# Perceiver stack of four layers: x of the cross attentions turned by VectorE's blocks and through DRAM instead of by TensorE

## The chip, the cores and the metric

One core of a Trainium2 chip runs the whole program. TensorE multiplies matrices (and can turn a 128x128 tile by multiplying it with the identity), VectorE, ScalarE and GpSimd work elementwise, and SyncE (SP) issues the DMAs. The engines each run their own stream of instructions in order and wait for each other by semaphores. The metric is the device time of one execution in microseconds; the smaller the better.

## The reference

The input x is 64 sequences of 64 tokens with 128 features; a context of 64 x 128 x 96 and a mask come with it. Four layers follow one another, each with a cross attention to the context, a self attention and a feed forward part (in layers 0, 2 and 3 one that routes tokens to experts). Every part starts with a layer norm of x and adds its result to x. What the change touches is the start of three cross attentions:

```python
# layer 0 (x is the visual side, ctx the text side); the result has 128 columns, one for a context row
xn = layernorm(x)                                        # each token over its 128 features
v = einsum('bsd,hd->bsh', xn, Wv) + bv                   # 64 features
t = einsum('bsd,hd->bsh', ctx, Wt) + bt
x = x + einsum('bih,bjh->bij', v, t) / maximum(norm(v)[:, :, None] * norm(t)[:, None, :], 1e-8)
# layers 2 and 3: attention with 16 heads of 8 features
q = layernorm(x) @ Wq + bq ;  k = ctx @ Wk + bk ;  val = ctx @ Wv + bv
x = x + project(softmax(q k^T / sqrt(8)) val)            # layer 2 also clips the scores; layer 3 projects by a small MLP
```

TensorE contracts over partitions. x lies in SBUF with tokens on partitions, so for q the normed x has to be turned, so that its features lie on partitions (for the first product of layer 0 as well).

## The kernel before, in words

x stays in SBUF from first to last, 32 tiles of 128 tokens. Each of the 12 parts ("blocks", L0x, L0a, L0f, L1x, ... L3f; x is a cross attention, a a self attention, f a feed forward) is cut into jobs, mostly of 4 tiles (512 tokens), so 8 jobs for each of L0x, L2x and L3x, 24 in all. Two contexts, each with its own rooms in SBUF and four of the eight PSUM banks, take one job after another by PLAN. Their jobs run interleaved on the same engines, so that the one fills the other's waits.

A job is a set of programs, one for an engine, cut into steps by `yield`. The order in which all steps of both contexts are issued is a string written out in the code, ORDER, of 8,321 characters: a letter is the next step of one program (small letters context 0, capitals context 1), a digit ahead of a letter of TensorE's is a number of filler matmuls, identity times a constant, that the step issues where it has `pe_warm` (L467), and a plus loads the weights of a later block. Since each engine works in order, a wait in one step holds back all that the string puts behind it on that engine, the other context's steps too.

Each job has main programs (PROGRAMS: p for TensorE, a for ScalarE, g for GpSimd, v for VectorE) and early ones (EARLY_PROGRAMS), which may run while the job before in that context is still at work: d, VectorE's sums of the norm (L501); l, GpSimd's power of -1/2 (L489); k, ScalarE's normed x, written to xn (L509); and q, the DMA of the context, ctxT (L530). Each context has two early rooms, used in turn.

The main part of L2x and L3x starts with `pe_context` (L1875). TensorE makes the keys (L1882) and the values (L1887) from ctxT, then turns the four tiles of xn with four transposes into one PSUM bank (`pe_turn`, L463). ScalarE copies the bank to SBUF as xT (`act_turned`, L479), in act_context (L1900). TensorE then multiplies xT with wq (L1897), ScalarE adds the bias. Meanwhile VectorE spreads the keys over four lanes into kx (L1768) and adds the bias to the values, va (L1931, L2062). In L3x it makes qx from q as well. In L0x it is the same with other names: pe_L0x (L542) multiplies ctxT (L552), turns xn, and multiplies xT with wv (L564). Both routines also use `pe_turn` and a bank elsewhere; only the turn of xn is touched.

The expert blocks use SP for another thing: the routing weights are written to DRAM (`sp_keep`, L847) and read back spread over the partitions (L865, L879, L882). These are the s steps.

Of the kernel before, what the change touches and what calls it, by code (L numbers as in the profile page):

```python
# [12 lines left out]
P = 128  # L13
S = 64
D = 128
CX = 96
SC = 128
# [223 lines left out]
class Context:  # L241
# [4 lines left out]
    def __init__(self, nc, number, psum):  # L246
        self.nc, self.number, self.psum = nc, number, psum
        self.named, self.tally = {}, {}
# [21 lines left out]
class Job:  # L270
# [3 lines left out]
    def __init__(self, core, k, name, group, context, turn, first):  # L274
        self.core, self.k, self.name, self.group, self.context, self.turn, self.first = core, k, name, group, context, turn, first
        self.tiles = TILES.get(name, 4)
        self.seqs, self.tok, self.ctok = 2 * self.tiles, self.tiles * P, 2 * self.tiles * SC
        self.psum, self.c, self.half = context.psum, core.c, core.half
        self.m = {**core.rooms[name][context.number], **core.early_rooms[name][context.number][turn % 2]}
        self.x = core.x[:, group * self.tiles:(group + 1) * self.tiles, :]  # L280
        self.warm = 0
        self.base = {n: count for n, count in context.tally.items() if n[:-1] in EARLY}
# [41 lines left out]
    def free_early(self, engine, source=False):  # L324
# [5 lines left out]
        for number, count in done.items():  # L330
            if count > 0:
                engine.wait_ge(self.core.contexts[number].sem("done"), count)

# [187 lines left out]

def early_room(r):
# [19 lines left out]
def pe_L0x(nc, j):  # L542
# [45 lines left out]
def act_L0x(nc, j):  # L588
# [6 lines left out]
    yield  # L595
    s.wait_ge(*j.at("turned", 1))
    act_turned(nc, j, m["xT"][:], 0).then_inc(*j.up("features"))
# [1277 lines left out]
def pe_context(nc, j):  # L1875
# [15 lines left out]
    t.wait_ge(*j.at("normed", 1))  # L1891
    t.wait_ge(*j.at("k_ready", 1))
    pe_turn(nc, j, 0, m["xn"])
    yield
    pe_warm(nc, j, 1)
    t.wait_ge(*j.at("features", 1))
    t.matmul(psum[:, 1, :], j.weight("wq"), m["xT"][:], start=True, stop=True).then_inc(*j.up("queries"))  # L1897


def act_context(nc, j):  # L1900
# [6 lines left out]
    yield  # L1907
    s.wait_ge(*j.at("turned", 1))
    act_turned(nc, j, m["xT"][:], 0).then_inc(*j.up("features"))
# [34 lines left out]
def pe_L2x(nc, j):  # L1944
# [8 lines left out]
    t.wait_ge(*j.at("features", 2))  # L1953
# [51 lines left out]
def act_L2x(nc, j):  # L2005
    yield from act_context(nc, j)
    yield
    nc.scalar.wait_ge(*j.at("turned", 2))
# [113 lines left out]
def act_L3x(nc, j):  # L2122
    s, m = nc.scalar, j.m
    yield from act_context(nc, j)
    yield from act_waves(nc, j, SC, 1)
# [677 lines left out]
def sp_L3f(nc, j):  # L2803
# [18 lines left out]
EARLY_PROGRAMS.update({name: {"q": sp_early_context, "d": dve_early, "l": pool_early, "k": act_early} for name in ("L0x", "L2x", "L3x")})  # L2822
# [11 lines left out]
EARLY_BYTES = 6528  # L2834

# [5 lines left out]
    "vqQDDddDVdldkdddp8paglPLaDKQqDpDDLPaApgApGp7PvvdDavAkGKvvpPPP1paVVa3pgdAdaVpgdVlVPp1pA2PGvQvA4PDadvAkPGPlPvdvkV1pVa3pDDA"  # L2841
    "dLdvvDavvadavlVKpVvVPPAApGQPvvvA1PlvGvPvvdPDgkdVv9pVgAaVVVPpApGpapaDpaDLapDKQppvvpPaApDvavvaPavDkdpddDLA1PvlGpPvDvKvPvVV"
    "vAvvVgldVvVP5PAG1pAQDPapDAGPPaPpVDVLpgAVaaVDVPppakppKDpDDdvLvp1PaApDAGvva4PavavApkGPvPdpdPvvvVdvlVvAKVvvVgVLv+P1pVgAPaVD"
    "AVVApAVpdKDPpVpaaDPkpVVDaVLpapDVKVpVvVvGpLVa4pdPDpbArdrpKrdrlrPrrrGPrrrPrrArPArAPrArrPrrPaPVdvVPcApbPsaDVsVApAVsADpVDsvp"
    "LPsavgpVpgaPvgcVVgVpVcaVkcVpVGcVpvPaDpgApKvLPgaPGPPAAPAPAPPVDVPpApPaVVAcAAcpKDVVvDgPvgcVcPv1pVVVaVpVpbVpVdGpaDrLrVpavPGr"
    "pArrrLPrdrrPDrArrPKrrDdrlPrrAPrrrAvPAPPacVbVPpAspKDvPsaVsDVADpdsLAVpAVspvDgPagpVgpaKvgPcVgkVVpVcaVpVcVGcVcvGPvpAgPagPPAL"
    "APAPAPPPVVPpAcvPgVDAVVcAAVcKvpPqdDapVpbrPrrrarpVrVrprrdrvpardVplrvpaVprvprVarpvparVrprdVrGrvpaVcpbDvsPaDpdLApvsGDdPsdPAl"
    "PsAdPAsKPgPkPgAcgPacgkVcVgc+DPgpAcvgDcgPPBRRcdRRDRAcLRRPvRPqRRdpVPaRARpRpRRaRPdRdRRRpDvvCVpBASaaPgaSPvgVPSAlvPVSPAvgPSVP"
    "APVGvPAvPGdPpGpapaCaVGACkGpCGvCVGvdaCGCKvCddvlCVPpAaPvDpdBRPaRkRDpRRRDRvpapRpRadqRRdpRaRRRgpdRRRARRadvPaCVgPBvSPlAvPdvkV"
    "gSdPAPVSPALSvPvpdSpVapaPdaGApVGCvGCvaPGPlvvPGDApaPdvAkVpGPapAvppadqdapddvlpadVgpaGvPaCVKgdCGvCvdCgCCvvV1PAppapaakpPvPdvl"  # L2850
    "aPPvv1pBRRadvdpRRRARRAPVakRpVvpPaqdRpRAdDpaRdpRalRvgRRpaRDddRPDRaRdRdCVgPvBSlPvAvPgVSPAPVSPAvSvppdapSaPaGk1pGCvPGvaCGCvv"
    "GCVApaLCvVGpPGakpvpPAdqdavpDdpVadlpaGdpaKdgdvCaCgCvvVPAgDPdDPBDRPRRLvARvplpaRpRaPdRaRVkpRRRARPvPRRvRaPDRVRPRRvRvCdApBaPS"
    "vkpSapSvppaVApqdaddlpaSdgVpavGSvPGaPAgPvCAvdkgPdKVCdVPPlAvvpGpdapaPaGpAGCvGCvVaCGCvvCpaPvkpa1pvppadqdapvddVpaGpagvCaVPgA"
    "1PQlvvPgBRDPRRdPdAkdAv3pvpRaVpaPRaRRRpDRDLPvPvRaRVRDPdlvv1pdRAaPvkVpRdRPDaDpRDLDvppaapRARRvKpdapdaVgARvCaPBgPVSPAvKPvVSg"
    "DPdSSlv9pvSpapaPaGA1pAGCvGCvaGPCGvdvGpaCvkpa1pvvpdCaVpdGVpvGCvCvCvgV+VPgpQADdaPvPvDPpDvAVpAAGPvgAlvpGLVpaVdDpVGaapVp1PvP"
    "ADpkVDvAvPvvA2PvpVpaKpaappvVDvALvv6pVVDvpPaKpVpAvpvPvAvgPdgpddvV4PPAaDPQvDPvVADpAAPvGADvpLGDpaDgpVDaDVLaVpGpv3plvVvv5PvA"
    "vpVpPaDdPApAa1PapVpVAvkvvVv7pDVvpPaKpVKpvAvPvAvPgV1PpQDAgpPvPavDPvVApAAPvDvpLgDpaADGpGVadapVdpVGv3pDvvDvLV3PvPAvpdVplaPA"
    "pAa1PapVpVAvDdvkvv6pDVVvpPaApVpvPvAKvPpKvgVPQvgAPDPDDvaLPpDvdApAAPvGKvpdpVaDAdpDlVaGapVVdpGv3pvvVDvL3PvgPDvpVpaPApAAa1Pa"
    "pVpVAvvkvVv9pVPvADpVavdKpvvvPaavvAvvPvvvvdvvvdvVPPAAPlvQDPvAvvDvDpvLAPaGDvdpAvKVpGVVpVaDGkvDpapVVPPDvApgPvpLaAgApPvagpVp"
    "VvApDgpVVpvvvpPaApKVvvvPDaavvA1PvvvvvdvvvVPPAAPvQvPvAvvvGDpPDavAvDdLvVVpADvvpGVpVaGpapVvpVgPvPAPADpgaDADdlpadPkvgpVpVLvA"  # L2860
    "pgpKVDVpDvvvpPaKpVAvvvPdaavvAvdPvvvvvvvvdVPPAAPlvQvvPvAvvVGvDpAPavVDpAvDpGLVpDVvaGDpapVdDVPpAvPDgvPApALakgPpVapVvApDgpKV"
    "VDPvAgpVKPpAPVPAvvvpPPAaPADqGPADVdpVADddvGvvalVavvVvGvvvvvvvvvvvvvLVp1PvaVDvpvAvPPdApAPapVvVpApvaVgVKppkvgPaApVaPvgpApvP"
    "gpV+DPpVADp2PvvPVvVqpVVGPapPVGvVApVDvLagPv1pVaVPg3PdnAPzmAzzPwy6nwwAdPyVny2nVxVPdzlzV2mVG1nxVmzxmwzw3mzPyw7PwwAnxP3mynxy"
    "mnx2mAzznwDAPzKPw6mzVVVVwPzwVPAyPwPdVxnVPyVmVGnxDVGymDVx2mAnPww1mDzLzV4nGwPwwzx7mzzVy5nxVPDymnxmynwPwzzApPakpAvpAqddPaPp"
# [12 lines left out]
    "PrrvrrrrarrdVPrprAvPrkVGkPpAcpa1PabVspAvvsNpZspaMZZpQavYWggcvgWcgcWGcXcNvDpdYMdNXYMaNX1MZZNWWDMZ1pZZaWpYWWpavXNvpdvlY3Mv"
    "lgvNXgaMY1NXMWZW2MDZvNgWpLWWppZXp2MZdZYpvXNvMYvX3MaNWWvMYpWNaZWZ2NWaXZpZZMvYppv1NvXvvvpYMvDvNvXMYKNW1pWZZPvA2PgvVPvDgvPA"
# [213 lines left out]
```

## Time and profile before

| | us |
|---|---|
| three runs, median | 2554.51 |
| lowest and highest run | 2552.6, 2557.82 |
| profiled execution, span from the first to the last instruction | 2557.4 |
| TensorE busy | 2254.9 (88%) |
| VectorE busy | 1746.6 (68%) |
| ScalarE busy | 1368.6 (54%) |
| GpSimd busy | 774.0 (30%) |

The profiled execution has no other time on its page than its span; it lies inside the spread of the runs. A busy share is that of the whole span, over blocks with different limits. TensorE's contains the fillers (L471, 588 of them). L0x runs from about 20 to 130 us, L2x from 787 to 1433, L3x from 1632 to 2298; other blocks run beside them. The mean granted clock of TensorE is 0.971 of full speed.

### The profile page before, as it was taken

To read this page: it belongs to the slowest core of one execution; us is meant where nothing else is said; L and a number is where in the kernel's file an instruction comes from. 1 tells how busy PE (TensorE), PEld (TensorE's weight loads), DVE (VectorE), ACT (ScalarE), POOL (GpSimd) and SP (SyncE) were. 2 spreads that over 40 slices of the span, in tenths; PEclk is the share of its full clock that TensorE was granted. 3 is DMA by queue.
4 is the path that set the end of the run, shared out by engine and by line. 5 is a ranking of instruction groups with operands and counts; after the bars stand their busy time and mean duration, and the time that the engine had idled before them with its cause. 6 is when DMAs were issued, how large, how long until landed. Compare 5 with 4: busy or idle time off the path is not lost.

```text
span 2557.4 us, 62072 instructions
## 1 busy us (share of the span) xinstructions
PE 2254.9 (88%) x26420; PEld 1506.9 (59%) x26556; DVE 1746.6 (68%) x4832; ACT 1368.6 (54%) x2287; POOL 774.0 (30%) x676
## 2 busy tenths in 40 slices
PE   5889999877988888998888888888988889999999
PEld 3556666655565554565655666665656556555666
DVE  5775666577667777676777778777767674556642
ACT  4667676545555665545666544344455544555542
POOL 3323446432342212122222122211223223323443
PEclk9999999989999999999999999999999989999999
DMA  3011313100000000010000000000000102121132
GB/s 115 19 41 34 80 45 75 42 24 9 9 11 14 8 8 6 1 47 10 17 16 10 19 25 25 25 16 17 10 11 16 58 8 71 40 55 54 55 104 62
DMA packets 50452, 84.14 MB, mean 33 GB/s; under 512 B 9536, under 2 KB 24768, under 8 KB 49792
## 3 DMA queue, kind: packets, MB, share of 16 engines
q1 hardware_dynamic: 50176, 80.18, 11.3%
q8 instruction: 208, 3.41, 0.6%
q14 instruction: 68, 0.56, 0.1%
HBM read 77.54 MB, written 2.62 MB: 31 GB/s over the span
## 4 chain that ended last, share of the span: by engine, by line
PE 57%; DVE 25%; ACT 8%; issue 4%; POOL 3%; DMA 1%; SPq 1%; another core or an unknown queue 0%; DVEq 0%; POOLq 0%; ACTq 0%
PE psum L946 6%; PE psum L908 5%; PE psum L904 5%; PE psum L1606 3%; PE psum L463 2%; DVE c_L3x_most L1726 2%; PE psum L1699 2%; DVE c_L2x_mx L2081 2%; PE psum L1984 2%; DVE c_L2x_p L2087 1%; PE psum L471 1%; PE psum L1395 1%; PE psum L1976 1%; PE psum L773 1%; PE psum L778 1%
## 5 line engine op out<-in xcount | busy, mean ns | idle before, releaser
L893 POOL TENSOR_TENSOR c_L3f_h<-c_L3f_h,c_L3f_spread 128x512 f32<-128x512 f32 x96 | 121.3, 1283 | 188.8 <-DMA c_L3f_spread<-scratch 103.1
L471 PE MATMUL psum<-halves_held 128*128 128x512 bf16 x454 | 131.0, 403 | 14.0 <-issue 9.8
L936 DVE TENSOR_TENSOR c_L3f_h<-c_L3f_h,psum 128x512 f32<-128x512 f32 (+1 forms) x112 | 75.9, 682 | 76.5 <-PE psum L908 52.0
L922 ACT ACTIVATE c_L3f_h<-psum 128x512 f32<-128x512 f32 (+1 forms) x112 | 65.5, 594 | 110.2 <-PE psum L904 99.1
L946 PEld LDWEIGHTS psum<-weights,c_L3f_h 128*128 128x128 f32 (+1 forms) x896 | 108.1, 193 | 19.3 <-issue 15.3
L946 PE MATMUL psum<-weights,c_L3f_h 128*128 128x128 f32 (+1 forms) x896 | 112.9, 279 | 0.0
L904 PE MATMUL psum<-c_L3f_xT,weights 128*128 128x512 f32 x208 | 107.4, 601 | 0.0
L908 PE MATMUL psum<-c_L3f_xT,weights 128*128 128x512 f32 x208 | 107.4, 603 | 0.0
L471 PEld LDWEIGHTS psum<-halves_held 128*128 128x128 bf16 x588 | 54.3, 102 | 74.8 <-issue 35.1
L893 POOL TENSOR_TENSOR c_L0f_h<-c_L0f_h,c_L0f_spread 128x512 f32<-128x512 f32 x64 | 82.5, 1313 | 50.4 <-DVE c_L0f_h L936 39.2
L1606 PE MATMUL psum<-c_L3x_qx,c_L3x_kT 32*128 32x256 f32 x512 | 77.1, 427 | 21.1 <-DVE c_L3x_most L1726 17.4
L2020 ACT ACTIVATE c_L2x_p<-c_L2x_p 128x1024 f32<-128x1024 f32 x64 | 67.5, 1055 | 46.9 <-DVE c_L2x_p L2087 46.6
L2081 DVE TENSOR_REDUCE c_L2x_mx<-psum 128x8 f32<-128x1024 f32 x64 | 77.9, 1219 | 15.0 <-PE psum L1976 14.2
L893 POOL TENSOR_TENSOR c_L2f_h<-c_L2f_h,c_L2f_spread 128x256 f32<-128x256 f32 x64 | 45.7, 740 | 137.6 <-DMA c_L2f_spread<-scratch 134.5
L1984 PE MATMUL psum<-constants_held,c_L2x_p 128*128 128x128 f32 x512 | 67.6, 276 | 16.0 <-ACT c_L2x_p L2022 15.3
L2087 DVE SCALAR_TENSOR_TENSOR c_L2x_p<-psum,c_L2x_mx 128x1024 f32<-128x1024 f32 x64 | 78.1, 1221 | 1.4
L1984 PEld LDWEIGHTS psum<-constants_held,c_L2x_p 128*128 128x128 f32 x512 | 56.6, 141 | 33.5 <-issue 17.5
L1726 DVE TENSOR_REDUCE c_L3x_most<-psum 128x16 f32<-128x2048 f32 x32 | 73.0, 2282 | 4.5 <-PE psum L1596 4.3
L1606 PEld LDWEIGHTS psum<-c_L3x_qx,c_L3x_kT 32*128 32x128 f32 x512 | 46.1, 197 | 50.1 <-DVE c_L3x_most L1726 29.7
L1976 PE MATMUL psum<-c_L2x_kx,c_L2x_qT 32*64 32x512 f32 x512 | 65.4, 639 | 8.7 <-DVE c_L2x_va L2062 5.5
L2025 ACT COPY c_L2x_pT<-psum 128x1024 f32<-128x1024 f32 x64 | 63.9, 1007 | 16.6 <-PE psum L1984 16.5
L922 ACT ACT_TABLE_LOAD x56 | 71.8, 1283 | 1.0
(640 smaller groups left out, 6520.0 us busy)
## 6 DMA issues: line engine op xcount, KB each, us to landing
c_L0f_spread<-scratch SPq DMA_DIRECT2D x64, 256.0 KB, 5.5
c_L3f_spread<-scratch SPq DMA_DIRECT2D x32, 512.0 KB, 5.3
c_L2f_spread<-scratch SPq DMA_DIRECT2D x64, 128.0 KB, 3.1
c_L3f_spread<-scratch SPq DMA_DIRECT2D x64, 128.0 KB, 5.8
c_L0x_ctxT<-ctxT SPq DMA_DIRECT2D x8, 384.0 KB, 7.8
c_L1x_ctx<-ctx SPq DMA_DIRECT2D x16, 192.0 KB, 2.4
c_L2x_ctxT<-ctxT SPq DMA_DIRECT2D x8, 384.0 KB, 3.6
c_L3x_ctxT<-ctxT SPq DMA_DIRECT2D x8, 384.0 KB, 3.7
```

Of the source, the lines that this page charges most:

```text
L471: nc.tensor.matmul(j.psum[:, bank, :], j.half["ident"], j.half["take"], start=True, stop=True)
L893: nc.gpsimd.tensor_tensor(h, h, j.m["spread"][:, f, :], ALU.mult).then_inc(*j.up("mixed"))
L904: t.matmul(psum[:, 1 + 2 * f % 3, 0:j.tok], j.weight("gate")[:, cols], m["xT"][:], start=True, stop=True).then_inc(*j.up("gate"))
L908: t.matmul(psum[:, 1 + (2 * f + 1) % 3, 0:j.tok], j.weight("up")[:, cols], m["xT"][:], start=True, stop=True).then_inc(*j.up("inner"))
L922: nc.scalar.activation(j.m["h"][P - rows:P, f, :], j.psum[0:rows, 1 + 2 * f % 3, 0:j.tok], ACT.Silu).then_inc(*j.up("silu"))
L946: put = nc.tensor.matmul(j.psum[:, 0, k * P:(k + 1) * P], j.m["h"][rows, f, k * P:(k + 1) * P], j.weight("down")[rows, f * P:(f + 1) * P], ...
L1606: nc.tensor.matmul(j.psum[rows, g, at:at + 256].rearrange("p (j q) -> p j q", j=QUAD), j.m["kT"][f, s * keys:(s + 1) * keys], j.m["qx"][f, ...
L1726: put = v.tensor_reduce(m["most"][:, u, :].rearrange("p (g j) -> p g j", j=QUAD), psum[:, :, u * QUAD * keys:(u + 1) * QUAD * keys].rearra ...
L1976: put = t.matmul(psum[64 * r:64 * r + 64, g, :].rearrange("p (j k) -> p j k", j=QUAD), m["qT"][f, s * S:(s + 1) * S], m["kx"][f, :, s * SC ...
L1984: put = t.transpose(psum[:, n // 4, (n % 4) * P:(n % 4 + 1) * P], m["p"][:, n * P:(n + 1) * P], j.c["ident"])
L2081: v.tensor_reduce(mx, s, AX, ALU.max).then_inc(*j.up(lane_name("max", h)))
L2087: v.scalar_tensor_tensor(p, s, -limit, bcast(mx, 2, SC), ALU.max, ALU.subtract).then_inc(*j.up(lane_name("low", h)))
```

## The change

For the 24 jobs of L0x, L2x and L3x, the normed x is no longer turned by TensorE's four transposes and ScalarE's copy. It is turned ahead of the job, in the early programs. VectorE turns all 32x32 blocks of xn in one instruction, into a new room of 2 KB per partition and context ("blocks"). SP writes that room to DRAM (256 KB) and, once that has landed, reads it back in four DMAs, one for each group of 32 features, in runs of 512 bytes, so that the blocks come to lie with all 128 features on partitions. They land in xn's own room. TensorE's query matmul reads them through a rearranged view and waits for the DMAs. That takes one step each from TensorE's and ScalarE's main programs (in L0x the filler call ahead of the turn as well as the wait for xn), adds one to d and two to q. The order string is new in all its length; PLAN is unchanged. Its fillers number 584 (before 588): L2x 208 (218), L3x 75 (93), L1x 58 (42), L0x 39 (38).

```diff
+def dve_blocks(nc, j, i, x, at=0):
+    n, width = x.shape[1], x.shape[2]
+    v = nc.vector
+    v.wait_ge(*j.at("normed", i))
+    j.free_blocks(v)
+    out = j.m["blocks"][:, at:at + n * width].rearrange("p (b t q) -> p b t q", t=n, q=32)
+    v.transpose(out, x[:].rearrange("p t (b f) -> p b t f", f=32)).then_inc(*j.up("shift"))
+
+def sp_blocks(nc, j, shift, width, ctx=None):
+    if ctx is not None:
+        nc.sync.wait_ge(*j.at("ctx", ctx))
+    nc.sync.wait_ge(*j.at("shift", shift))
+    nc.sync.dma_start(j.core.turns[j.context.number][:, 0:width], j.m["blocks"][:, 0:width]).then_inc(*j.up("ctx", 16))
+
+def sp_features(nc, j, written, out, n, at=0):
+    nc.sync.wait_ge(*j.at("ctx", written))
+    width = out.shape[0]
+    held = j.core.turns[j.context.number][:, at:at + n * width].rearrange("(a f) (b c) -> b f a c", a=4, c=32 * n)
+    for b in range(width // 32):
+        nc.sync.dma_start(out[32 * b:32 * b + 32, :].rearrange("f (a c) -> f a c", a=4), held[b]).then_inc(*j.up("ctx", 16))
+    j.take_blocks("ctx")
+
+def dve_early_context(nc, j):
+    yield from dve_early(nc, j)
+    yield
+    dve_blocks(nc, j, 1, j.m["xn"])
 def sp_early_context(nc, j):
     yield
     j.free_early(nc.sync)
     nc.sync.dma_start(j.m["ctxT"][:], j.core.ctxT[:, bass.ts(j.group, j.ctok)]).then_inc(*j.up("ctx", 16))
+    yield
+    sp_blocks(nc, j, 2, 4 * D, 16)
+    yield
+    sp_features(nc, j, 32, flat(j.m["xn"]), 4)
...
@@ pe_L0x
     j.halves(t)
-    pe_warm(nc, j, 1)
-    t.wait_ge(*j.at("normed", 1))
     if not j.first:
         t.wait_ge(*j.at("resid", 0))
-    pe_turn(nc, j, 0, m["xn"])
-    yield
     pe_warm(nc, j, 1)
-    t.wait_ge(*j.at("features", 1))
-    t.matmul(psum[0:64, 1, :], j.weight("wv"), m["xT"][:], start=True, stop=True).then_inc(*j.up("queries"))
+    t.wait_ge(*j.at("ctx", 16 + LANDED))
+    xT = features(flat(m["xn"]))
+    t.matmul(wide(psum[0:64, 1, :], xT), j.weight("wv"), xT, start=True, stop=True).then_inc(*j.up("queries"))
@@ pe_context
-    t.wait_ge(*j.at("normed", 1))
     t.wait_ge(*j.at("k_ready", 1))
-    pe_turn(nc, j, 0, m["xn"])
-    yield
     pe_warm(nc, j, 1)
-    t.wait_ge(*j.at("features", 1))
-    t.matmul(psum[:, 1, :], j.weight("wq"), m["xT"][:], start=True, stop=True).then_inc(*j.up("queries"))
+    t.wait_ge(*j.at("ctx", 16 + LANDED))
+    xT = features(flat(m["xn"]))
+    t.matmul(wide(psum[:, 1, :], xT), j.weight("wq"), xT, start=True, stop=True).then_inc(*j.up("queries"))
@@ act_context (and the same in act_L0x)
-    s.wait_ge(*j.at("turned", 1))
-    act_turned(nc, j, m["xT"][:], 0).then_inc(*j.up("features"))
-    yield
```

LANDED is 16 + 4 x 16, one write and four reads at 16 each. The helpers `flat`, `features` and `wide` are views only.

## Rows read from the trace of the kernel before

**Rows 1.** The page's head, its busy times and its chain by engine.
```profile
span 2557.4 us, 62072 instructions
...
PE 2254.9 (88%) x26420; PEld 1506.9 (59%) x26556; DVE 1746.6 (68%) x4832; ACT 1368.6 (54%) x2287; POOL 774.0 (30%) x676
...
PE 57%; DVE 25%; ACT 8%; issue 4%; POOL 3%; DMA 1%; SPq 1%; another core or an unknown queue 0%; DVEq 0%; POOLq 0%; ACTq 0%
```
**Rows 2.** Windows: stretch, length, busy of PE, PEld, DVE, ACT, POOL, clock, DMA, GB/s.
```profile
787.00:1433.00 646.00, 556.30 (x8121) 360.82 (x8180) 478.33 (x1129) 386.44 (x565) 134.02 (x121) 0.98 0.04 13
...
1632.00:2298.00 666.00, 589.93 (x8127) 385.51 (x8156) 460.44 (x1165) 320.23 (x490) 163.15 (x152) 0.95 0.10 29
```
**Rows 3.** Pieces of the chain at job starts: start us, us, what.
```profile
32.64 0.63 PE psum L463 x4
...
43.23 0.60 PE psum L463 x4
43.82 0.65 PE psum L471 x3
...
125.91 0.47 ACT c_L0x_xT L479
...
860.93 0.59 PE psum L463 x4
861.52 0.86 PE psum L471 x4
...
1235.33 0.44 PE psum L463 x4
...
2245.94 0.44 PE psum L463 x4
```
**Rows 4.** Pieces of the chain at the second job of L3x.
```profile
1694.03 3.65 DVE c_L3x_kx L1768 x4
1697.68 1.13 DVE c_L3x_va L1931
1698.81 1.59 DVE c_L3x_qx L1768 x4
```
**Rows 5.** Line 463, the transposes: duration ns min/median/max, first and last start.
```profile
L463 PE MATMUL psum<-constants_held,c_L3x_xn x32: 270/272/275, 1632.3 to 2246.1; 128*128 128x128 f32 x32
```
**Rows 6.** Line 479, ScalarE's copy of the turned x, the same columns.
```profile
L479 ACT COPY c_L3x_xT<-psum x8: 561/585/586, 1632.9 to 2246.4; 128x512 f32<-128x512 f32 x8
```
**Rows 7.** VectorE's block transposes: two by line 1762, one by groups (mean ns).
```profile
L1762 DVE STREAM_TRANSPOSE c_L3x_xT<-c_L3x_att x32: 295/311/313, 1649.7 to 2297.5; 128x128 f32<-128x128 f32 x32
L1762 DVE STREAM_TRANSPOSE c_L1a_xT<-c_L1a_att x16: 435/445/446, 534.2 to 980.3; 128x256 f32<-128x256 f32 x16
...
L1751 DVE STREAM_TRANSPOSE c_L3x_oT<-psum 128x512 f32<-128x512 f32 x32 | 22.9, 715 | 63.3 <-PE psum L1699 63.2
```
**Rows 8.** DMA issues, median us from issue to landing; then SP's issue times (ns).
```profile
c_L0f_spread<-scratch SPq DMA_DIRECT2D x64, 256.0 KB, 5.5
...
c_L3x_ctxT<-ctxT SPq DMA_DIRECT2D x8, 384.0 KB, 3.7
...
out<-x_held SPq DMA_DIRECT2D x8, 256.0 KB, 2.3
...
L533 SPq DMA_DIRECT2D c_L2x_ctxT<-ctxT x8: 312/328/598, 748.5 to 1309.3; - x8
...
L2809 SPq DMA_DIRECT2D out<-x_held x8: 383/384/384, 2159.6 to 2555.1; - x8
```
**Rows 9.** Timeline at two job starts: start us, us, instruction.
```profile
18.36 1.65 ACT L424 ACTIVATE c_L0x_xn<-x_held,c_L0x_norm_shift,c_L0x_norm_rstd 128x128 f32<-128x128 f32 x4 [16.34 <-DVE c_L0x_norm_shift L417]
...
30.07 1.02 PE L564 MATMUL psum<-c_L0x_xT,weights 128*64 128x512 f32 x2
...
1135.58 1.64 ACT L424 ACTIVATE c_L2x_xn<-x_held,c_L2x_norm_shift,c_L2x_norm_rstd 128x128 f32<-128x128 f32 x4
...
1141.83 1.02 PE L1897 MATMUL psum<-c_L2x_xT,weights 128*128 128x512 f32 x2
```

More of the change, by code:

```diff
@@ L247, in __init__ @@
         self.nc, self.number, self.psum = nc, number, psum
-        self.named, self.tally = {}, {}
+        self.named, self.tally, self.taken = {}, {}, None
     def sem(self, name):
@@ L278, in __init__ @@
         self.psum, self.c, self.half = context.psum, core.c, core.half
-        self.m = {**core.rooms[name][context.number], **core.early_rooms[name][context.number][turn % 2]}
+        self.m = {**core.rooms[name][context.number], **core.early_rooms[name][context.number][turn % 2], "blocks": core.blocks[context.number]}
         self.x = core.x[:, group * self.tiles:(group + 1) * self.tiles, :]
-        self.warm = 0
+        self.warm, self.taken = 0, context.taken
         self.base = {n: count for n, count in context.tally.items() if n[:-1] in EARLY}
@@ L332, in free_early, with free_blocks, take_blocks @@
                 engine.wait_ge(self.core.contexts[number].sem("done"), count)
+    def free_blocks(self, engine):
+        if self.taken:
+            engine.wait_ge(*self.taken)
+    def take_blocks(self, name):
+        full = self.full(name)
+        self.context.taken = (self.context.sem(full), self.context.tally[full])
     def begin(self, engine):
@@ L519, in act_early_twice, with flat, features, wide @@
         act_norm(nc, j, 2, j.m[once], j.x, j.m["norm"][2][:, 1, :], j.m["norm"][3][:, 1, :])
+def flat(ap):
+    return ap[:].rearrange("p t d -> p (t d)")
+def features(ap):
+    return ap.rearrange("p (a t q) -> p t a q", a=4, q=32)
+def wide(out, like):
+    return out if len(like.shape) == 2 else out.rearrange("p (t a q) -> p t a q", a=4, q=32)
+def dve_blocks(nc, j, i, x, at=0):
[17 more added lines that the diff above has]
+    j.take_blocks("ctx")
+LANDED = 16 + 4 * 16
 def early_room(r):
@@ L2124, in act_L3x @@
     yield from act_context(nc, j)
-    yield from act_waves(nc, j, SC, 1)
+    yield from act_waves(nc, j, SC, 0)
     for f in range(2):
@@ L2834 @@
 EARLY_BYTES = 6528
+TURN_BYTES = 2048
 PLAN = (
@@ L2949, with build @@
     pass
-def build(nc, n_seq, weights, constants, halves, x, ctxT, ctx_tok, mask, out, scratch, blocks):
+def build(nc, n_seq, weights, constants, halves, x, ctxT, ctx_tok, mask, out, scratch, turns, blocks):
     core = Core()
-    core.nc, core.scratch = nc, scratch
+    core.nc, core.scratch, core.turns = nc, scratch, turns
     core.places, _ = weight_places(weight_table())
@@ L2981, in build @@
         widths = [0]
+        core.blocks = []
         core.rooms, core.early_rooms = {n: [] for n in blocks}, {n: [] for n in blocks}
         for number in range(CONTEXTS):
-            start = -(-nc.sbuf_base // 64) * 64 + number * (max(widths) + 2 * EARLY_BYTES)
+            start = -(-nc.sbuf_base // 64) * 64 + number * (max(widths) + 2 * EARLY_BYTES + TURN_BYTES)
+            core.blocks.append(Room(nc, f"c{number}_turn", start + 2 * EARLY_BYTES).tile("blocks", P, TURN_BYTES // 4))
             for name in blocks:
@@ L2988, in build @@
                 assert early[0].at <= start + EARLY_BYTES
[L2989 removed]
+                room = Room(nc, f"c{number}_{name}", start + 2 * EARLY_BYTES + TURN_BYTES)
                 core.rooms[name].append(ROOMS[name](room))
[L2991 removed]
+                widths.append(-(-(room.at - start - 2 * EARLY_BYTES - TURN_BYTES) // 64) * 64)
         core.weights_in = [nc.alloc_semaphore(f"weights_in{k}") for k in range(SLOTS)]
@@ L3064, in program @@
           dram("out", (n_seq * S, D), kind="ExternalOutput"),
-          [dram(f"scratch{k}", (EXPERTS0, 4 * P), kind="Internal") for k in range(CONTEXTS)], blocks)
+          [dram(f"scratch{k}", (EXPERTS0, 4 * P), kind="Internal") for k in range(CONTEXTS)],
+          [dram(f"turns{k}", (P, TURN_BYTES // 4), kind="Internal") for k in range(CONTEXTS)], blocks)
 def kernel(**inputs):
```

153 lines of the change are left out of this document (74 added, 79 removed).

## The prediction

> **What bounds the kernel now.** I read the page's head and its chain first. The chain is 57% TensorE, 25% VectorE and 8% ScalarE [rows 1], so an item of TensorE's is worth a bit over half its length, one of VectorE's a quarter, one of ScalarE's a twelfth, as long as nothing else is known of its place. TensorE's 88% busy is not all work: 588 filler matmuls stand in the order (the digits), put where TensorE would wait. Then I read the stages by windows: in that of layer 2's cross attention VectorE is busy 478 of 646 us, in that of layer 3's 460 of 666, against TensorE's 556 and 590 [rows 2]. TensorE leads, VectorE is near behind. Last I followed the chain through the start of each of the 24 changed jobs. At nine of them it holds the turn or the copy behind it [rows 3]. At nine others it runs through VectorE instead, as at 1694: four multiplications into kx, then va, then qx, with the turn, the copy and the query matmul all done beside it [rows 4]. So what limits a start is as often VectorE as TensorE.
>
> **Removed.** Per job four transposes on TensorE. One lasts 272 ns, but they overlap [rows 5]. What four cost together is seen in the chain where TensorE runs without a gap: 0.44 us [rows 3]. 24 x 0.44 = 10.6 us. Then the ScalarE copy of 128x512, 0.585 us [rows 6]: 24 x 0.585 = 14.0 us. By the chain's shares this is 10.6 x 0.57 + 14.0 x 0.08 = 6.0 + 1.1 = 7.1 us. The second way to count is by what the chain itself holds: 0.63 at 32.6, 0.60 + 0.65 at 43.2 (turn, then fillers until the copy is done), 0.47 at 125.9, 0.59 + 0.86 at 860.9 (again turn and fillers), and five turns of 0.44 (1235, 1821, 2071, 2177, 2246): 6.0 us [rows 3]. The two agree; I take 6.5 us. What is late next in those places is the query matmul itself, behind the values.
>
> **Added on VectorE.** One block transpose of 128x512 per job. The trace has no such transpose from SBUF to SBUF with this pattern. It has 311 ns for 128x128 and 445 for 128x256, a slope of 134 ns per 128 columns, so 311 + 3 x 134 = 713; the one of 128x512 out of PSUM takes 715 ns; four of 128x128, should the 4x4 pattern break it up, are 1.24 us [rows 7]. I take 0.715: 24 x 0.715 = 17.2 us. At VectorE's share of the chain that is 17.2 x 0.25 = 4.3 us. Bounds: 0 if each falls into a gap (VectorE idles in a quarter of these stages) and 24 x 1.24 = 29.8 us if the long price holds and all of it is on the path. It is an early step, with freedom of place, so I take 2.5 us, between nothing and the share.
>
> The Trainium skill speaks against this change: VectorE: DVE Perf Modes, Rules for kernel authors, says to use TensorE for a 128x128 transpose when PSUM will do as its target, and VectorE for blocks of 32x32. Its table in The three transpose paths has 311 ns for VectorE and 390 for TensorE at 128x128 in bf16. The trace has the same 311 ns in f32, but only 0.44 us for four transposes on TensorE; so by instruction time alone the rule is right here, and a sum by it would end at 17.2 us of VectorE for 10.6 us of TensorE, a loss if both were worth the same.
>
> **Added on the DMA queues.** Per job a 256 KB write to DRAM and four reads of 64 KB in rows of 512 bytes: five more issues on SP. An issue takes 328 to 384 ns [rows 8], so 120 x 0.35 = 42 us of SP, which otherwise only waits. The trip from a finished xn: 0.7 transpose; write issued and landed, 2.3 us as the 256 KB of the output; three more issues ahead of the last read, 1.0; that read, 2.4 to 3.7 [rows 8]; with the waits some 6.5 to 8.5 us, and with short rows as much as 9. No compute engine waits in it until the query matmul. Before, the shortest lead of layers 2 and 3 was that at 1135.58 + 1.64 to 1141.83, 4.6 us [rows 9]. In the new order the letters from the ScalarE step that makes xn (k) to the query step are 16 to 44 in layer 0 (12 to 40 before), 24 to 37 in six jobs of layer 2 and 23 in one of layer 3. A letter is on average 2557.4 / 8321 = 0.31 us, so 24 letters are 7.4 us: the trip just fits. Should it be 1 us late, kx and va (3.65 + 1.13 us [rows 4]) are still running beside it, and q isn't wanted until they are done. I take zero. What that cover would not hide: the query step stands in TensorE's order ahead of the other context's steps, so a late landing halts both contexts.
>
> What is queued behind the two new waits of SP: the reads wait for the write's landing (about 2.5 us), the write for the block transpose. Behind them stand ctxT of the next job, a weight load, and in three places the keep step of an expert spread (behind jobs 5 and 6 of layer 2 and job 6 of layer 3). Layer 0's spreads land 5.5 us after issue [rows 8], so 2.5 us more is a modest part of their lead; I take zero, with 3 x 2.5 = 7.5 us as the other end. At the kernel's start the trip is hidden: xn of the first job is ready at 18.36 + 1.65 = 20.0 and the query runs at 30.1, since its context is late [rows 9], so 10 us are there for 7 to 9. The query's operand is now read in three strides of 32 elements; no row has that view. Its bounds are nothing and a doubling of the pair that takes 1.02 us [rows 9], 24 us in all; I take zero, since its runs are whole blocks of 32 elements, and the outer end stays with the range's upper half. The 2 KB of room per context and the wait for its last reader cost nothing.
>
> **Order anew.** All 8,300 letters are placed again. Its fillers: 584 against 588 (layer 2's cross attention 208 for 218, layer 3's 75 for 93, layer 1's 58 for 42). Fillers stand where TensorE would wait, so the gaps that they cover haven't grown, while its work is 10.6 us less. If the gaps without fillers also stay, the span falls by 10.6 + 4 x 0.2 = 11.4 us; that is the far end. The near end is the sum with the shares, 7.1 - 4.3 = 2.8. A new order may as well lose: there is no row for it, and I put 8 us on both sides of its effect. I take 7 us between the ends, the 6.5 - 2.5 = 4 of the terms and 3 more for the refitted order.
>
> **The sum.** The profiled execution spans 2557.4 us, 2.9 above the median of the three runs (2554.5) and inside their spread. 2557.4 - 7 = 2550.4 in the profile, 2547.5 as a median; 0.27% faster.
>
> **Rivals.** (1) Nothing measurable: the removed work was beside the path and VectorE gives back what is saved; 7.1 - 4.3 = 2.8 us, about 2552. For it: the starts led by VectorE [rows 4]. Against: TensorE leads in both stages [rows 2].
> (2) The trip through DRAM is late, slower. Place: the seven job starts just named. If write and reads land in 5.5 us each, as layer 0's spreads from scratch do [rows 8], the trip is 0.7 + 5.5 + 1.0 + 5.5 = 12.7 us, 4.7 late, 3 of it covered by kx, so 1.7 for each of seven starts, 12 us, less the 2.8: about 2563.5. It decides from a trip of 11 us on. Against: 256 KB to DRAM land in 2.3 us, and those stages move 13 to 29 GB/s [rows 2, 8].
> (3) VectorE becomes the bound: three quarters of the 17.2 us on the path, 12.9 - 7.1 = 5.8, about 2560. For it: 74% busy in layer 2's stage. It decides where the block transpose lies between the end of one job and kx of the next, which is where the new order puts it in layer 2.
> (4) The change doesn't do what it says, some of the turns staying: excluded by the diff; 0.01.
>
> The Trainium skill, DMA: Bandwidth & Descriptors, Latency and other measured facts, puts a DMA's fixed cost at about 2 us. By it an estimate for the two legs is 4 us and the moving of 512 KB; the output's 2.3 us agrees, and this weighs against rival 2.
>
> **How the numbers follow.** Forecast 0.45, rival 1 0.28, rival 2 0.12, rival 3 0.14, rival 4 0.01. A measurement of this kernel tells no less than 0.2% (5.1 us) from no change: faster 0.45, same 0.29, slower 0.26. The forecast's own range is 2541 to 2549; with the unknown of the order and the rivals the range for 8 in 10 is 2537 to 2562.
>
> **What would show it.** Right: 96 transposes and 24 copies fewer; TensorE's busy time about 10 us less; the first query of a layer 2 job directly behind its values, and no wait of TensorE on a DMA above 1 us; block transposes at 0.7 us. Wrong: rows in which TensorE waits for xn's DMA; VectorE's share of the chain above 27%; a query matmul above 0.6 us; spreads waiting behind SP; or a difference outside the cross attentions, which would be the order's alone.

## The result and the profile after

| | before | after |
|---|---|---|
| runs of the comparison, median (lowest to highest), us | 2556.16 (2552.6 to 2557.84), 4 | 2579.99 (2575.87 to 2582.52), 4 |
| span of the profiled execution, us | 2557.4 | 2578.7 |
| mean granted clock of TensorE | 0.971 | 0.971 |

The ratio is 1.0088, 95% interval 1.0069 to 1.0107: 0.9% slower, where 0.27% faster was forecast, and outside the range. The intervals here and below are at 95%. The page of the kernel after, head, busy times and chain by engine, against [rows 1]:

```profile
span 2578.7 us, 62168 instructions
...
PE 2267.6 (88%) x26456; PEld 1499.2 (58%) x26456; DVE 1765.0 (68%) x4856; ACT 1354.4 (53%) x2262; POOL 779.9 (30%) x676
...
PE 61%; DVE 22%; ACT 10%; issue 3%; POOL 3%; DMA 1%; SPq 1%; DVEq 0%; ACTq 0%; POOLq 0%
```

VectorE has 18.4 us more, ScalarE 14.2 less, and there are 100 weight loads fewer (96 transposes, 4 fillers). TensorE's busy times can't be compared: before, 134 filler records are missing. VectorE's share of the chain fell, from 25% to 22%, and TensorE's rose. Below are the three kinds of new instructions by lines, and the query matmul that now reads the blocks, with what TensorE waited for ahead of it. The durations are in ns (least, median, most), then come the first and last start; for a DMA the duration is that of the issue, and the us to landing stand below it.

```profile
L554 DVE STREAM_TRANSPOSE c_turn_blocks<-c_L2x_xn x8: 703/711/712, 777.1 to 1382.6; 128x512 f32<-128x512 f32 x8
...
L562 SPq DMA_DIRECT2D turns<-c_turn_blocks x24: 326/344/543, 22.1 to 2239.1; - x24
...
DMA to landing us min/median/max: 2.0/2.2/7.8
...
L571 SPq DMA_DIRECT2D c_L2x_xn<-turns x32: 302/432/1028, 779.9 to 1386.7; - x32
...
DMA to landing us min/median/max: 1.7/1.9/4.6
...
L1955 PE MATMUL psum<-c_L2x_xn,weights x16: 591/592/1222, 792.5 to 1390.8; 128*128 128x512 f32 x16
...
  DMA c_L2x_xn<-turns: 4.3, 1
  DMA c_L3x_xn<-turns: 1.2, 2
```

So every new piece has, in the median, the size that was forecast, 0.71 us and 2.2 + 1.9 us, and the query matmul is no slower (median 592 ns, as before). TensorE waited for the trip three times in layers 2 and 3, 5.5 us in all, and in layer 0 another 4.6 (three times), waits of its weight loads counted. VectorE waited too: ten of the 24 block transposes found their xn not ready (idle us, times), 15.9 us in all, 5.9 of them in the kernel's first job. The forecast priced the busy time of this step and no wait of VectorE ahead of it.

```profile
  ACT c_L0x_xn L434: 10.3, 4
  ACT c_L2x_xn L434: 5.1, 5
  ACT c_L3x_xn L434: 0.5, 1
```

One wait of TensorE is far longer than the others. The timeline around it (start us, us, instruction, idle before it):

```profile
1141.45 0.35 SPq L3069 DMA_DIRECT2D weights<-weights  x1
1142.77 0.71 DVE L554 STREAM_TRANSPOSE c_turn_blocks<-c_L2x_xn 128x512 f32<-128x512 f32 x1 [1.32 <-ACT c_L2x_xn L434]
1143.55 0.34 SPq L562 DMA_DIRECT2D turns<-c_turn_blocks  x1
...
1151.35 1.75 SPq L571 DMA_DIRECT2D c_L2x_xn<-turns  x4
...
1154.74 1.98 PE L1955 MATMUL psum<-c_L2x_xn,weights 128*128 128x512 f32 x2 [4.35 <-DMA c_L2x_xn<-turns]
```

And the DMAs issued from 1135 to 1160 (KB each, us to landing):

```profile
weights<-weights SPq DMA_DIRECT2D x1, 2121.0 KB, 7.8
c_L2x_ctxT<-ctxT SPq DMA_DIRECT2D x1, 384.0 KB, 3.5
turns<-c_turn_blocks SPq DMA_DIRECT2D x1, 256.0 KB, 7.8
c_L2x_xn<-turns SPq DMA_DIRECT2D x4, 64.0 KB, 1.9
```

In job 4 of L2x the trip is issued 2 us behind a weight load of 2.1 MB, and its write lands 2 us after that has landed, 7.8 us after its issue and not 2.2. The lead was there: from the finished xn at 1142.8 to the query's turn on TensorE at 1150.4 are 7.6 us, but the trip took 12. (Five other writes of this profile took 3.8 to 5.1 us.) The Trainium skill, DMA: Bandwidth & Descriptors, Queues, rings and completion order, says that each DMA engine takes the descriptors of a ring in the order of the ring; the 7.8 us beside the load's 7.8 agree.

The stages of [rows 2], moved to where they lie now, with the same columns:

```profile
787.40:1450.00 662.60, 571.86 (x8136) 365.46 (x8135) 490.33 (x1132) 381.44 (x555) 135.96 (x121) 0.96 0.06 18
1649.80:2323.00 673.20, 586.91 (x8122) 380.33 (x8121) 460.55 (x1176) 316.46 (x484) 162.42 (x151) 0.96 0.12 35
```

Layer 2's takes 16.6 us more and layer 3's 7.2. To follow the loss through all kernels I took the ends of the last write of some jobs to x. Lag behind the kernel before, us, in the profiled executions (again is `after_again`, old+new `oldorder_new`, late `oldorder_late`, and so on; these kernels come in the next section):

```
end of (us before)       after again nowait nodmas early noturn(new) old+new late noturn(old) swap1 swap2
L0x job 7      143.8      +4.2  +2.6  +2.3   +1.9   +2.8    +2.7     +24.8   -1.0   -1.4    +10.1  +6.0
L1f job 3      782.5      +0.4  +0.8  +2.2   +1.3   +2.8    +6.5     +24.8   -4.1   +1.2     +9.9  +1.8
L1f job 7     1132.3      +9.1  +5.6  +7.1   +3.8   +7.6   +12.9     +25.8   -3.6   +2.5    +10.3  +3.6
L2f job 0     1180.6     +14.5 +18.3  +6.4   +4.2   +6.8   +13.3     +26.7   +1.0   +2.8    +10.4  +4.3
L2f job 4     1434.6     +17.1 +16.3  +3.7   +1.8   +4.3   +14.3     +31.9   +6.8   +2.5    +10.8  +5.2
L2f job 15    1978.6     +26.1 +28.0 +15.8  +10.3  +15.4   +23.3     +40.5  +21.3   +9.7    +20.0 +12.0
L3a job 7     2436.5     +21.1 +22.3 +13.4   +5.1  +10.8   +17.4     +40.2  +34.4   +8.0    +25.0 +13.6
```

Each column is one execution, so differences of a few us between columns say little. Two columns mislead: the profiled execution of `after_nodmas` is the fastest of its six, 9.8 us under their median, and that of `neworder_noturn` is 5 us over its median. By their ratios these two stand the other way round.

### The profile page after: what moved, and what is told of

Its sections match the earlier page's. It is cut to its first block, busy times and chain, and to the rows that moved or that the text cites. A ratio compares the mean times of both kernels' runs of the same rounds, so it can differ in the third digit from the quotient of the medians.

```text
span 2578.7 us, 62168 instructions
## 1 busy us (share of the span) xinstructions
PE 2267.6 (88%) x26456; PEld 1499.2 (58%) x26456; DVE 1765.0 (68%) x4856; ACT 1354.4 (53%) x2262; POOL 779.9 (30%) x676
## 4 chain that ended last, share of the span: by engine, by line
PE 61%; DVE 22%; ACT 10%; issue 3%; POOL 3%; DMA 1%; SPq 1%; DVEq 0%; ACTq 0%; POOLq 0%
PE psum L1006 6%; PE psum L968 5%; PE psum L964 4%; PE psum L1666 3%; PE psum L481 3%; PE psum L473 2%; PE psum L1759 2%; PE psum L2031 2%; PE psum L2039 2%; PE psum L1455 2%; DVE c_L3x_most L1786 2%; PE psum L1656 1%; DVE c_L2x_mx L2136 1%; DVE c_L2x_p L2142 1%; PE psum L1505 1%
## 5 line engine op out<-in xcount | busy, mean ns | idle before, releaser
L481 PE MATMUL psum<-halves_held 128*128 128x512 bf16 x584 | 171.7, 410 | 9.9 <-DVE c_L0x_r L698 5.6
L953 POOL TENSOR_TENSOR c_L2f_h<-c_L2f_h,c_L2f_spread 128x256 f32<-128x256 f32 x64 | 46.1, 742 | 152.6 <-DMA c_L2f_spread<-scratch 137.8
L2039 PEld LDWEIGHTS psum<-constants_held,c_L2x_p 128*128 128x128 f32 x512 | 60.0, 147 | 34.0 <-issue 19.7
```

What stands on the lines that cost most here:

```text
L481: nc.tensor.matmul(j.psum[:, bank, :], j.half["ident"], j.half["take"], start=True, stop=True)
L953: nc.gpsimd.tensor_tensor(h, h, j.m["spread"][:, f, :], ALU.mult).then_inc(*j.up("mixed"))
L2039: put = t.transpose(psum[:, n // 4, (n % 4) * P:(n % 4 + 1) * P], m["p"][:, n * P:(n + 1) * P], j.c["ident"])
```

## The experiments

Theories at the start: the trip's waits cost the time; VectorE's added work does; or the order does, since it was fitted to other work. Each ratio is to runs of the kernel before on the same chip, with its 95% interval.

**The two halves of the change apart.** `oldorder_new` keeps the old order and puts in the new mechanism, `neworder_old` keeps the new order and the old mechanism. Their new letters had to be placed by a rule.

```diff
oldorder_new (capitals: context 1)
-"vqQDDddDVdldkdddp8paglPLaDKQqDpDDL...
+"vqQDDddDVdldkdqqdddpaglPLDKDQQQqD8pDDL...
neworder_old
-"vdddDDDLldQkqdKqPAqdDD...
+"vdddDDDLldQkqKPPAAdDd...
```

> The new way of turning x in the order of the kernel before: the 24 turn steps and 24 copy steps are taken out of the old string, and the block transpose, the write and the reads are put in a few letters behind the step that makes xn. Theory A (the new order string costs the time, not the way of turning): about the kernel before or up to 5 us below it, 2548 to 2558. Theory B (the way of turning itself costs: VectorE waits for xn, SP's waits, the trip): slower by most of the 23 us, 2570 or more.

Measured: 2603.04 us, 1.0161 (1.0120 to 1.0202), so theory B by its number. 24.8 us were lost within L0x.

> The old way of turning x (four transposes on TensorE, a copy on ScalarE) in the new order string, the turn put right behind the values and the copy behind it. Theory A: still slow, 2575 to 2590, since the order stays and 10.6 us of TensorE come back. Theory B: back near the kernel before, under 2565.

Measured: 2607.07 us, 1.0178 (1.0141 to 1.0215); slower than either theory had it, with 25.0 us lost in L0x. Both crossings lose about twice what the whole change does. The likely reason, argued and not shown, is that each order was fitted to its own mechanism and letters placed by a rule fit neither; so these two can't tell the theories apart.

**The turning left out in either order.**

```diff
neworder_noturn (xn is read as it lies, in xT's place)
-    dve_blocks(nc, j, 1, j.m["xn"])
-    sp_blocks(nc, j, 2, 4 * D, 16)
-    sp_features(nc, j, 32, flat(j.m["xn"]), 4)
-    t.wait_ge(*j.at("ctx", 16 + LANDED))
+    t.wait_ge(*j.at("normed", 1))
oldorder_noturn
-    pe_turn(nc, j, 0, m["xn"])
-    act_turned(nc, j, m["xT"][:], 0).then_inc(*j.up("features"))
```

> The new order with all turning left out: no block transpose, no write, no reads; the query matmul reads the normed x as it lies, so its product is not the query. The difference to the changed kernel is the whole price of the new way of turning. Theory A: 2570 to 2580, within 8 us of the changed kernel. Theory B: 2560 or less.

Measured: 2571.0 us, 1.0025 (1.0000 to 1.0051), mean granted clock of the ten executions 0.973. The time is at the lower end of theory A, the ratio nearer to no change than to the kernel after.

> The old order with the turn and the copy left out (their steps stay, empty); the query matmul reads the normed x as it lies. The difference to the kernel before is all that taking the turn off TensorE and ScalarE can give. By the chain of the kernel before, 6.0 to 7.1 us: 2547 to 2550. If gaps are kept and the work alone goes, up to 11 us. If it gives nothing (2553 and more), the turn was beside the path everywhere.

Measured: 2567.71 us, 1.0028 (1.0010 to 1.0045), mean granted clock of the ten executions 0.967, against 0.972 in the 19 of the kernel before beside them. This is the strongest result of the study: 24.6 us of instructions taken away from TensorE and ScalarE, in the same order, made the kernel slower. My sum had these at 6.5 us of gain. With the turning left out the two orders are also equal, 1.0028 and 1.0025 on one chip: no cost of the new order as such is seen, within 0.3% either way.

The lower clock is a rival for why the removal gained nothing. From one execution of the kernel before to another the time moves with the granted clock; a straight line through its 64 executions, chip by chip, has 1.6 us for 0.001. By this estimate the 0.005 that are missing here go with 8 us, all of the loss. What made the clock fall isn't shown.

**The change's parts in the new order.** These three ran on one chip with `after_again`, which is the kernel after once more.

```diff
after_nowait (the trip goes on, into a spare room; nobody waits for it)
-    sp_features(nc, j, 32, flat(j.m["xn"]), 4)
+    sp_features(nc, j, 32, j.m["blocks"][:], 4)
-    t.wait_ge(*j.at("ctx", 16 + LANDED))
+    t.wait_ge(*j.at("normed", 1))
after_nodmas (block transposes only)
-    sp_blocks(...)
-    sp_features(...)
after_filled (against the gap at 783; see below)
+    if j.group == 4:                                   # L1a, behind the values
+        for _ in range(12):
+            t.matmul(psum[:, 3, :], j.half["ident"], j.half["take"], start=True, stop=True)
```

> The changed kernel once more, unchanged, so that the other three of this group are compared with it on one chip. All theories: 1.007 to 1.011 of the kernel before.

Measured: 2578.36 us, 1.0077 (1.0054 to 1.0100).

> The changed kernel with its block transposes, its writes and its reads, but the reads land in the spare room and the query matmul reads the normed x as it lies, so its product is not the query; nobody waits for the trip. Theory W (TensorE's waits for the trip cost): near the kernel with all turning left out, 1.000 to 1.004. Theory L (the load on VectorE and SP costs, or the order does): 1.006 or more.

Measured: 2572.51 us, 1.0051 (1.0031 to 1.0071), between theory W and theory L.

> The changed kernel with the block transposes on VectorE, but no write and no reads; the query matmul reads the normed x as it lies, so its product is not the query. If VectorE's 17 us and its waits for xn are the price, this is as slow as the changed kernel, 1.006 or more; if it is the waits of SP and the transfers, 1.002 to 1.004 as with all turning left out.

Measured: 2574.28 us, 1.0059 (1.0036 to 1.0082), just under the 1.006 that VectorE as the price would give. So no cost of the five DMAs of a job is seen while nobody waits for them, though they take 24 x (0.344 + 4 x 0.432) = 50 us of SP's time. Waiting for them costs 0.26% by the ratios of after_again and after_nowait, whose intervals overlap; the medians are 5.9 us apart. The table shows where: from L1f's job 7 to L2f's job 0 the kernel with the wait loses 12.7 us and that without it gains 0.7. That is three times the wait of 4.3 us that stands in the timeline of after_again, too:

```profile
1151.23 2.05 PE L1955 MATMUL psum<-c_L2x_xn,weights 128*128 128x512 f32 x2 [4.30 <-DMA c_L2x_xn<-turns]
```

The windows of this stretch, after_again (1137.90 to 1198.80) and after_nowait (columns as in [rows 2]):

```profile
1137.90:1198.80 60.90, 49.26 (x640) 32.52 (x640) 36.79 (x80) 24.51 (x38) 12.66 (x12) 0.83 0.15 52
```

```profile
1139.30:1187.00 47.70, 40.31 (x640) 27.23 (x640) 36.89 (x80) 24.55 (x38) 12.74 (x12) 1.00 0.20 67
```

The same 640 matmuls take 49.26 us busy and not 40.31, at a granted clock of 0.83: 2 x 0.17 x 60.9 = 20.7 us of it at 1.2 GHz, in one piece that begins at 1150 within the wait. TensorE was busy without a gap in it from 1151.3 to 1170.5, at 0.50. In the first profile of the change (`after`) only 3.4 us at 1.2 GHz follow this wait, but a piece of 27.3 us begins at 783. There TensorE had stood for 2.55 us until L1f's job 3 freed its context (the timeline of the kernel after, then its window, and last the same window of the kernel before):

```profile
782.96 3.75 PE L1942 MATMUL psum<-c_L2x_ctxT,weights 96*128 96x512 f32 x4 [2.55 <-issue]
...
782.90:837.70 54.80, 50.97 (x711) 28.18 (x711) 40.37 (x77) 26.74 (x36) 10.27 (x7) 0.75 0.04 9
```

```profile
782.50:829.90 47.40, 39.56 (x717) 23.25 (x725) 36.99 (x73) 26.12 (x35) 10.98 (x8) 1.00 0.04 11
```

That stretch took 7.4 us more than before. `after_filled` puts work into this gap.

> The changed kernel, all of its work, with 12 more fillers (2.6 us at the full clock) behind the values of the first L1a job of the second context, where TensorE stood still from 780.4 to 783.0 us before the clock was granted at half for 27.3 us. Theory C (the idle stretch that the new order has there costs the clock, and the clock 7 us): no long stretch at half clock behind it, the first L2x job done about 47 us after the last L1f job ahead of it, not 55, and 1.005 to 1.008 of the kernel before. If the fall is not tied to that gap: no change to the changed kernel, or a little slower.

Measured: 2580.25 us, 1.0088 (1.0065 to 1.0112). Theory C is not borne out: behind 783 there is now one piece of 6.8 us, that at 1150 is there (20.5 us), and the total is no better. Nor can the filled gap claim the shorter piece: after_again has the same gap of 2.55 us unfilled and only 3.4 and 13.7 us behind it.

**The wait at 1150.** Moving the weight load behind the trip, and both cures together:

```diff
after_plusq
-...A3paPG+QQDvD...
+...A3paPGQQ+DvD...
```

> The changed kernel with one letter of its order moved: the load of the next layer's weights on SyncE stands behind the write and the four reads of job 4 of L2x and not ahead of them. Theory A (in this job the trip stands behind that load, TensorE waits 4.35 us for it at 1150 to 1155 us, and in after_again and after_filled a 20.5 us stretch at half clock follows there): the write lands in about 2.2 us and not 7.8, the wait there goes, no half-clock stretch of over 10 us begins between 1145 and 1165, the lag behind the kernel before at the first piece of L2f (1181 us) is 6 to 9 us and not 14 to 18, the whole is 8 to 12 us less than after_again, 2566 to 2571, ratio 1.003 to 1.005. Theory B (the lag belongs to the order; this wait is one of many and another takes its place): the lag at L2f stays above 13 us and the ratio at 1.007 to 1.009.

Measured: 2581.75 us, 1.0081 (1.0055 to 1.0108): theory B by the ratio, though the lag at L2f's job 0 is 12.6 us, a little under its 13. The wait for the trip went, the write landed after 2.0 us, and a wait for the weights came, with a piece of 10.2 us at 1.2 GHz from 1152. Timeline of after_plusq:

```profile
1142.84 2.91 SPq L571 DMA_DIRECT2D c_L2x_xn<-turns  x4
1145.84 0.38 SPq L3069 DMA_DIRECT2D weights<-weights  x1
...
1153.55 1.97 PE L2286 MATMUL psum<-weights 128*128 128x64 f32 x8 [2.93 <-DMA weights<-weights]
```

> after_plusq and after_filled in one: the weight load moved behind the trip, and 12 fillers behind the value projections of L1a's group 4. Theory A (two places, each a gap of TensorE that a stretch at half clock follows, are what the change lost): neither stretch (783, 1150), about 2560 to 2566, ratio 0.999 to 1.003. Theory B (the half clock moves elsewhere, as it did when only the first place was filled): ratio 1.005 to 1.009, with a half-clock stretch of over 10 us at a place where after_again has none.

Measured: 2581.59 us, 1.0084 (1.0056 to 1.0111): theory B. So two transfers are wanted at one moment, when L1f's last job is done: the weights for the freed slot and the trip. The one behind is late. What remains is to have the trip over by then:

```diff
after_early (the early letters L D K D Q Q of job 4 of L2x, 27 to 36 letters ahead)
-dAPldApPVPGvPAVpvvkGvPAPpVaPVGpvpadGdPdLDPlPPVVvva1pavvaVdKpDkvPpA3paPG+QQDv
+dAPldALpPVPGvDPAVpvvkGvPKAPpVDaPVGpvQpaQdGdPdPlPPVVvva1pavvaVdpkvPpA3paPG+Dv
```

> The changed kernel with the early steps of one job, number 4 of L2x, moved ahead in the order: the small GpSimd step, ScalarE's xn, VectorE's block transpose and SyncE's write and reads are issued during L1f's last experts, so that the trip is over when the load of the weights of the next layer (whose place is unchanged) is issued. Theory A (at this place two transfers are wanted at one moment, and the one behind keeps TensorE waiting, 4.3 us for the trip, 2.9 us for the weights): neither wait, no half-clock stretch of over 10 us near 1150, a lag at L2f's first piece of 5 to 8 us as in after_nowait, the whole 2568 to 2574, ratio 1.004 to 1.006. Theory B (the price of the trip is spread over all 24 jobs): lag at L2f above 12 us, ratio 1.007 to 1.009.

Measured: 2573.71 us, 1.0058 (1.0038 to 1.0078). Its timeline:

```profile
1129.67 0.70 DVE L554 STREAM_TRANSPOSE c_turn_blocks<-c_L2x_xn 128x512 f32<-128x512 f32 x1
1130.45 0.34 SPq L562 DMA_DIRECT2D turns<-c_turn_blocks  x1
...
1140.00 0.35 SPq L3069 DMA_DIRECT2D weights<-weights  x1
...
1148.74 1.02 PE L1955 MATMUL psum<-c_L2x_xn,weights 128*128 128x512 f32 x2
```

No wait, a clock of 1.00 in this stretch, and a lag at L2f's job 0 of 6.8 us, as without the wait (6.4): theory A. It does the whole work and is 0.2 to 0.3% faster than the change by the ratios, whose intervals overlap, and still slower than before.

**What the order is worth.** `oldorder_late` is oldorder_new with L0x left as before.

```diff
+EARLY_PROGRAMS["L0x"] = {"q": sp_early_plain, "d": dve_early, "l": pool_early, "k": act_early}
```

> The kernel before in its own order, with the new way of turning in L2x and L3x alone; L0x is as before (TensorE turns, ScalarE copies). It is oldorder_new without its part in L0x, which was behind by 24.8 us already when L0x ended, and by 40 at 1978. Theory A (what oldorder_new lost sits in L0x, where a job has little in front of it that could hide 6 us from xn to the landed blocks): nothing lost before 783 us, in all 10 to 18 us behind, 2572 to 2580, ratio 1.004 to 1.007. Theory B (any insertion of the trip into the old order costs as much, in each of the stages): ratio over 1.012.

Measured: 2591.76 us, 1.0119 (1.0090 to 1.0147). Nothing was lost before 783, as theory A had it, but 38 us after 1132, where A had 18 at most: placed by a rule, the trip costs in the later stages too. The ratio lies below theory B's 1.012 by a hair.

```diff
oldorder_noturn_fill (in the place of each turn)
+    for _ in range(2):
+        t.matmul(psum[:, 1, :], j.half["ident"], j.half["take"], start=True, stop=True)
```

> oldorder_noturn (old order, turning and copy left out, the query projection reads xn as it lies) with two filler matmuls of 512 columns in the place of each turning left out, so that TensorE is as busy as before while ScalarE stays free of its 24 copies. Theory A (leaving the turning out gained nothing because TensorE then stands idle and more time is granted at half clock, 175.6 us against 149.7): half-clock time falls back to about 150 us and the kernel is 0 to 8 us faster than before, ratio 0.997 to 1.000. Theory B (the cover is elsewhere: neither these matmuls nor the copies bound anything, and a change of timing alone costs a few us): ratio 1.001 to 1.005 with or without the fillers.

Measured: 2567.8 us, 1.0030 (1.0010 to 1.0050): theory B by the ratio. It doesn't settle the rival, for the clock came back only in part: the mean of the twelve executions is 0.970, against 0.972 before, and that of the profiled one, 0.964, is the lowest of them.

The last two kernels do exactly the work of the kernel before. Twelve steps of cross-attention jobs change places with the next step of the same engine that belongs to the other context:

```diff
before_swap1 (one of twelve)
-"...DKQqDpDDLPaApgApG...
+"...DKQqDDDLPpaApgApG...
```

> The kernel before, with 12 swaps in its order: in 12 of the 24 cross-attention jobs, picked by a random number, one step of TensorE or ScalarE changes places with the next step of the same engine that belongs to the other context (at most 4 letters away). Work and mechanism are the same. Theory A (every interleaving near this one differs by a few tenths of a per cent, and the order before is a good one of them, so a disturbance costs 0.1 to 0.5%, about what leaving the turning out cost): ratio 1.001 to 1.006, 2562 to 2575. Theory B (the time does not hang on such swaps, and the 0.3% of oldorder_noturn have a cause of their own in the missing turning): ratio 0.999 to 1.001.

Measured: 2581.75 us, 1.0091 (1.0069 to 1.0114).

> As before_swap1, with another random number: 12 other swaps. Theory A: 1.001 to 1.006, and not the same as before_swap1's within the intervals. Theory B: 0.999 to 1.001.

Measured: 2569.65 us, 1.0039 (1.0024 to 1.0055). Theory A, and more than it had for the first: twelve swaps among 8,321 letters can cost as much as the whole change did. The first one's six executions have a mean clock of 0.966, against 0.973 before, the second one's twelve have 0.972.

## Why the prediction was wrong, step by step

The terms of the forecast beside what the ratios give for them, each the difference of two kernels (us of 2557; a gain is negative):

| term | forecast | measured | between |
|---|---|---|---|
| turn and copy removed | -6.5 | +7.2 | before, oldorder_noturn |
| new order | -3, 8 on both sides | -0.8 | oldorder_noturn, neworder_noturn |
| block transposes | +2.5 | +8.7 | neworder_noturn, after_nodmas (two chips) |
| DMAs, nobody waits | 0 | -2.0 | after_nodmas, after_nowait |
| waits for the trip | 0 | +6.6 | after_nowait, after_again |
| sum | -7 | +19.7 | 1.0077 |

The first line has an interval of +2.6 to +11.5; the others are uncertain by 8 us or so on both sides, by their two intervals.

- **Removed (6.5 us of gain): this is the step that failed most.** The sizes were right (96 transposes and 24 copies went), the worth was not: the same removal alone, in the old order, is 7.2 us slower and not 6.5 faster. The shares of the chain, and the pieces of the chain at job starts, say what the path held, not what is saved when a piece goes. Why nothing was saved stays open. The lower granted clock of oldorder_noturn is one candidate (above); the other is that leaving steps out disturbs a fitted order as a swap does.
- **Added on VectorE (2.5 us).** 0.71 us each as forecast, 24 x 0.71 = 17.0 us of the 18.4 that VectorE has more. Its price by after_nodmas against neworder_noturn, 1.0059 against 1.0025, is 0.34%, and as much again on both sides by the two intervals, so nothing to 18 us; it holds the 15.9 us of VectorE's waits for xn, which the sum had left out. Rival 3 isn't borne out by the chain: VectorE's share fell.
- **The DMAs (zero).** SP's issues and the queues: right, by after_nowait. The spreads too: GpSimd's wait for layer 3's went from 103.1 to 96.0 us, for layer 2's from 134.5 to 137.8. The trip takes 6 us in the ordinary case (xn of job 0 of L2x done at 777.1, landed at 783.3), a little under the 6.5 to 8.5 of the estimate. What failed is the sentence that names a weight load only as something behind the trip: in one job the trip was behind the load. I took the landing time from rows in which nothing large was ahead. Nor did the cover by kx and va help: TensorE stood for 4.35 us. Price 0.19 to 0.26% (after_again against after_early and after_nowait), 5 to 7 us. This is rival 2's mechanism, at one place and not at seven, and by a cause that it didn't name; the prediction's sign for it, rows with TensorE waiting for xn's DMA, did appear.
- **Order anew (3 us of gain, 8 on both sides).** With the turning left out, the old and the new order are equal (-0.8 us), which is inside this term's bounds; their clocks differ, though, 0.967 and 0.973, so two effects may cancel in it. The bonus for the count of fillers has no run that bears it out. What the swaps show is that the bounds were narrow for any change of this string: two random disturbances of twelve letters cost 10 and 22 us. That the removal, or the block transposes, cost by the same mechanism is argued and not shown.
- **The clock.** For the change as a whole it is no cause of its own: 0.971 before and after, so about 150 us of each execution are at 1.2 GHz. It multiplies single gaps (12.7 us for a wait of 4.3) and gives back elsewhere. For oldorder_noturn it is 176 us at 1.2 GHz in the profile against 150; whether that is the cause or a result of its 0.28% stays open.

## What to carry to other kernels

In a kernel whose engines all work by one fitted order, measure first what a small disturbance of the order costs: a few random swaps give the spread (here 0.4 and 0.9%) that a saving of 0.3% has to beat. A share of the chain is no estimate of what removing a piece brings; the cheap test is a kernel that only leaves the piece out, in the old order, before the replacement is built (its result is false, its time is not). Here it would have shown that there was nothing to gain. When a step is moved from an engine to the DMA queue, look for every large transfer that may stand ahead of it on the same queue at the time when it is needed, and take the landing time from there.

## What the runs showed of the hardware

- A 256 KB write issued 2.1 us behind a load of 2,121 KB on the same queue landed after 7.8 us; issued ahead of the load it took 2.0 (after_plusq, after_early), and the median is 2.2. In the other order the load was the late one, and TensorE waited 2.93 us for it.
- An idle gap of TensorE of 4.3 us (1150) was followed by 20.5 us at 1.2 GHz in after_again, 19.2 of them with TensorE busy throughout, and the same gap of 4.35 us by 3.4 us only in after. The gap of 2.55 us at 783 was followed by 27.3 us in after and by 3.4 and 13.7 us in after_again. The stretches around the two long pieces took 7 and 13 us more than the ones they are compared with, and which gap is followed by a long piece changes from one execution to another.
- From one execution of the same kernel to another the time goes with the mean granted clock: on one chip the kernel before took 2551.9 us at 0.976 and 2573.4 at 0.966.
- A transpose of all 32x32 blocks of a 128x512 tile, SBUF to SBUF, takes 0.71 us on VectorE, and a matmul that reads its operand in runs of 32 elements takes the same 0.592 us as a plain one.
